# Cross-attention by Gram matrices: first loads, first batch and last row reordered, with fourteen unused products ahead of the first context

## The reference

```python
g = g_w @ c + g_b;  theta = theta_w @ x + theta_b;  phi = phi_w @ c + phi_b
W = theta.T @ phi / N
y = (W @ g.T).T
wy = w_w @ y + w_b
out = bn_gamma * (wy - bn_mean) * rsqrt(bn_var + 1e-5) + bn_beta + x
```

## Time and profile before

| | |
|---|---|
| median of 3 runs | 789.84 us (789.63 to 790.43) |
| profiled execution | 790.07 us |
| its span, first to last instruction | 788.3 us |
| PE busy | 772.0 us, 98% of the span |
| DVE, ACT, POOL busy | 498.1, 303.7, 527.5 us |
| moved by DMA | 103.17 MB, 131 GB/s over the span |
| granted TensorE clock, mean | 0.999 |

### The profile page before, as it was taken

The page is one execution under the profiler, slowest core; times in us unless marked ns, Lnnn a source line. Parts: engine busy times, 40 slices in busy tenths (PEclk is TensorE's granted clock), DMA queues, the critical chain, the costliest instruction groups (busy, mean ns, idle before and its releaser), DMA issues.

```text
span 788.3 us, 11592 instructions
## 1 busy us (share of the span) xinstructions
PE 772.0 (98%) x4045; PEld 666.7 (85%) x4045; DVE 498.1 (63%) x889; ACT 303.7 (39%) x514; POOL 527.5 (67%) x358
## 2 busy tenths in 40 slices
PE   4999999999999999999999999999999999999997
PEld 4688888888888888888888888888888888888886
DVE  3796574847657496574847657496574847657254
ACT  3634542325334243542325334243542325334131
POOL 4969785767857578585767857578585767857400
PEclk9999999999999999999999999999999999999999
DMA  9828254181733707255181733707255181730202
GB/s 237 197 108 214 107 129 192 35 226 62 178 142 74 246 0 213 106 124 195 33 228 58 178 142 72 247 0 213 106 121 198 32 228 60 178 143 1 107 1 106
DMA packets 55127, 103.17 MB, mean 131 GB/s; under 512 B 2474, under 2 KB 37956, under 8 KB 55108
## 3 DMA queue, kind: packets, MB, share of 16 engines
q1 hardware_dynamic: 52976, 101.86, 44.2%
q10 hardware_dynamic: 2132, 1.05, 0.8%
HBM read 69.35 MB, written 33.55 MB: 131 GB/s over the span
## 4 chain that ended last, share of the span: by engine, by line
PE 96%; DVE 1%; DMA 1%; ACT 1%; issue 0%; DVEq 0%; SPq 0%
PE wbank L667 57%; PE gbank L667 37%; PE wbank L830 1%; DMA ctx_sb<-in_ctx_dram 1%; PE wbank L708 1%; DVE x_sb L486 0%; PE wbank L686 0%; PE wbank L714 0%; ACT x_sb L366 0%; DVE tmp L509 0%; DVE tmp L508 0%; ACT x_hi L340 0%; DVE junk L590 0%; DVE x_sb L657 0%; DVE th_lo L583 0%
## 5 line engine op out<-in xcount | busy, mean ns | idle before, releaser
L286 POOL TENSOR_TENSOR ctxT_lo<-ctxT,ctxT_hi 128x512 fp32r<-128x512 f32 x124 | 167.2, 1349 | 205.7 <-ACT ctxT_hi L340 205.7
L297 POOL TENSOR_TENSOR ctx_sum<-ctx_sum,ctxT 128x512 f32<-128x512 f32 x108 | 157.0, 1454 | 0.2
L315 POOL TENSOR_TENSOR x_lo<-x_sb,x_hi 128x1024 fp32r<-128x1024 f32 x60 | 142.3, 2403 | 0.0
L340 ACT ACTIVATE mt<-wbank 128x512 fp32r<-128x512 f32 x64 | 37.9, 597 | 236.6 <-PE wbank L667 236.6
L657 DVE SCALAR_TENSOR_TENSOR x_sb<-wbank,const,x_sb 128x512 f32<-128x512 f32 x112 | 78.9, 747 | 73.1 <-PE wbank L667 73.1
L667 PE MATMUL wbank<-ctxT_lo,ctxT_hi 128*128 128x512 f32 x512 | 121.6, 393 | 0.0
L518 DVE TENSOR_TENSOR stage<-gbank,mt 128x384 f32<-128x384 f32 x64 | 28.3, 486 | 139.7 <-PE gbank L667 139.7
L667 PEld LDWEIGHTS wbank<-ctxT_lo,ctxT_hi 128*128 128x128 f32 x512 | 95.5, 190 | 18.7 <-POOL ctxT_lo L286 0.2
L340 ACT ACTIVATE ctxT_hi<-ctxT 128x512 fp32r<-128x512 f32 x124 | 76.5, 628 | 88.1 <-DVE ctxT L486 88.1
L667 PE MATMUL gbank<-ctxT_hi 128*128 128x384 f32 (+1 forms) x512 | 80.8, 314 | 10.1 <-ACT ctxT_hi L340 10.1
L667 PEld LDWEIGHTS gbank<-ctxT_hi 128*128 128x128 f32 x512 | 80.0, 191 | 12.0 <-issue 10.1
(11 more groups left out here) (107 smaller groups left out, 1327.4 us busy)
## 6 DMA issues: line engine op xcount, KB each, us to landing
x_sb<-in_x_dram SPq DMA_DIRECT2D x16, 2048.0 KB, 7.8
out_dram<-x_sb SPq DMA_DIRECT2D x64, 512.0 KB, 2.6
ctx_sb<-in_ctx_dram SPq DMA_DIRECT2D x60, 512.0 KB, 8.4
ctx_sb<-in_ctx_dram ACTq DMA_DIRECT2D x4, 256.0 KB, 7.1
ctx_sb<-in_ctx_dram SPq DMA_DIRECT2D x4, 256.0 KB, 7.2
x_sb<-in_L_xattn_w_w_dram SPq DMA_DIRECT2D x1, 512.0 KB, 11.7
stage<-in_L_xattn_theta_w_dram SPq DMA_DIRECT2D x1, 512.0 KB, 12.5
phi_nat<-in_L_xattn_phi_w_dram SPq DMA_DIRECT2D x1, 512.0 KB, 12.7
```

What stands on the lines that cost most here:

```text
L286: nc.gpsimd.tensor_tensor(ctxT_lo[:, c, :], turned_ctx(b, c), f(ctxT_hi[:, c, :]), ALU.subtract).then_inc(sem_, 1)
L297: nc.gpsimd.tensor_tensor(ctx_sum[:, :], ctx_sum[:, :], src, ALU.add).then_inc(ctxT_used, 1)
L315: nc.gpsimd.tensor_tensor(x_lo[:, k, :], x_sb[par][:, k, :], f(x_hi[:, k, :]), ALU.subtract).then_inc(x_lo_made, 1)
L340: nc.scalar.activation(dst, src, ACT.Copy).then_inc(sem_, 1)
```

## The change

The first context's loads are split otherwise between the two queues and go ahead of all vectors but two. gamma and var of the batch norm are loaded first, to rows of their own, turned by PE at once (`turn_norm`) and used from PSUM, so that the scale is made before the context is there. The other six vectors are loaded and turned later, after chunk 4. x of batch 0 is loaded right behind w_w. PE does 14 products of 128 x 512 ones whose result nobody reads, before it waits for the first context. DVE takes a second of the four first low parts of x from POOL. The context of batch 1 is transposed and split after T (chunks 0 to 3), after theta(1) (4 and 5) and among the first output rows (6 and 7). In the last batch the last output row is made, added up and stored in three pieces of 512, 256 and 256 columns, products of one piece after the other.

```diff
+    WARM_UP = 14
     NW = 5
...
         p1 = sb("p1", [P, KI])
-        vec_rows = sb("vec_rows", [5 * KC + 3 * KI, P])
-        vec_cols = sb("vec_cols", [P, 5 * KC + 3 * KI])
-        bt_col, bp_col, bg_col = (vec_cols[:, 5 * KC + i * KI:5 * KC + (i + 1) * KI] for i in range(3))
+        vec_rows = sb("vec_rows", [3 * KC + 3 * KI, P])
+        vec_cols = sb("vec_cols", [P, 3 * KC + 3 * KI])
+        bt_col, bp_col, bg_col = (vec_cols[:, 3 * KC + i * KI:3 * KC + (i + 1) * KI] for i in range(3))
         nbp_col = sb("nbp_col", [P, KI])
...
+        norm_rows = x_sb[1][0:2 * KC, 3, 0:P]
         theta_nat = stage[:, 0:KI * C].rearrange("p (k c) -> p k c", k=KI)
...
-        VECTORS = (w_b, bn_gamma, bn_beta, bn_mean, bn_var, theta_b, phi_b, g_b)
+        VECTORS = (w_b, bn_beta, bn_mean, theta_b, phi_b, g_b)
...
         W_BANK = [wbank[3], wbank[4]]
+        NORM_BANK = VEC_BANK = wbank[3]
         TP_BANK = [wbank[1], wbank[2], wbank[0], wbank[3]]
...
+        LAST_PIECES = [(0, HALF, wbank[1]), (HALF, HALF // 2, wbank[2]), (HALF + HALF // 2, HALF // 2, wbank[3])]
         OUT_BANK = [[wbank[1], wbank[2]], [wbank[3], gbank[0]], [wbank[4], wbank[0]], [wbank[1], wbank[2]]]
...
         vec_step = sem("vec_step")
-        vec_turned = sem("vec_turned")
+        vec_turned, vec_taken = sem("vec_turned"), sem("vec_taken")
+        in_norm, norm_turned = sem("in_norm"), sem("norm_turned")
         root_done, scale_made = sem("root_done"), sem("scale_made")
...
-            load_first_ctx(sp, (0, 2), 0)
-            load_vectors(sp, range(0, 4))
-            load_first_ctx(sp, (0, 2), 1)
+            sp.dma_start(norm_rows[KC:2 * KC, :], bn_var.rearrange("(m p) -> m p", p=P)).then_inc(in_norm, 16)
+            load_first_ctx(sp, (0, 1), 0)
+            load_first_ctx(sp, (0, 1), 1)
+            load_vectors(sp, range(0, 3))
             sp.dma_start(w_nat, w_w.rearrange("(m p) c -> p m c", p=P)).then_inc(in_w1, 16)
+            load_x(0, 0)
             sp.dma_start(theta_nat, theta_w.rearrange("(k p) c -> p k c", p=P)).then_inc(in_w4, 16)
             sp.dma_start(phi_nat[:, :, :], phi_w.rearrange("(k p) c -> p k c", p=P)).then_inc(in_w3, 16)
-            load_x(0, 0)
             sp.dma_start(g_nat, g_w.rearrange("(k p) c -> p k c", p=P)).then_inc(in_w2, 16)
...
                     load_ctx(b + 2)
-                for m in range(KC):
+                for m in range(KC if nxt else KC - 1):
                     sp.wait_ge(work_free, NO * b + NH * (m + 1))
                     sp.dma_start(out[b].rearrange("(m p) n -> m p n", p=P)[m], x_sb[par][:, m, :]).then_inc(stored, 16)
+                if not nxt:
+                    m = KC - 1
+                    for i, (a, n, bank) in enumerate(LAST_PIECES):
+                        sp.wait_ge(work_free, NO * b + (NH * m + i + 1))
+                        sp.dma_start(out[b].rearrange("(m p) n -> p m n", p=P)[:, m, a:a + n],
+                                     x_sb[par][:, m, a:a + n]).then_inc(stored, 16)
                 if nxt2:
...
             batches(sp, body)
-            sp.wait_ge(stored, 16 * KC * B)
+            sp.wait_ge(stored, 16 * (KC * B - 1 + len(LAST_PIECES)))
...
             nc.gpsimd.memset(ones_r[:, :].bitcast(F32), 1.0).then_inc(ones_done, 1)
+            nc.gpsimd.memset(x_hi[:, 0, 0:HALF].bitcast(F32), 1.0).then_inc(ones_done, 1)
...
             sum_rest(0)
-            for k in range(1, KC):
+            for k in (2, 3):
                 pool.wait_ge(x_hi_made, k + 1)
...
-            load_first_ctx(act, (1, 3), 0)
-            load_vectors(act, range(4, 8))
-            load_first_ctx(act, (1, 3), 1)
+            act.dma_start(norm_rows[0:KC, :], bn_gamma.rearrange("(m p) -> m p", p=P)).then_inc(in_norm, 16)
+            load_first_ctx(act, (2, 3), 0)
             act.wait_ge(ident_done, 2)
             nc.scalar.activation(tmp[:, 7, :], ident[:, 0:KC], ACT.Sqrt)
+            load_first_ctx(act, (2, 3), 1)
+            act.wait_ge(vec_step, 1)
+            nc.scalar.activation(tmp[:, 1, :], tmp[:, 0, :], ACT.Sqrt).then_inc(root_done, 1)
+            load_vectors(act, range(3, 6))
             hi(ident_r[:, :], ident[:, :], ident_r_made)
...
                 ctx_hi(0, c)
-                if c == 3:
-                    act.wait_ge(vec_step, 2)
-                    nc.scalar.activation(tmp[:, 1, :], tmp[:, 0, :], ACT.Sqrt).then_inc(root_done, 1)
...
             act.wait_ge(ones_done, 1)
+            act.wait_ge(vec_taken, 1)
             for k in range(KI):
...
                        LOW_BANK[g][:, 0:3 * P].rearrange("p (j c) -> p j c", j=3), low_hi_made)
-                if first(b):
-                    next_hi(0)
-                    next_hi(1)
-                    next_hi(2)
...
-                next_hi(3)
+                if not first(b):
+                    next_hi(3)
                 theta(0)
...
                 if first(b):
-                    next_hi(4)
-                    next_hi(5)
-                next_hi(6)
-                next_hi(7)
+                    for c in range(RING):
+                        next_hi(c)
+                else:
+                    next_hi(6)
+                    next_hi(7)
                 for k in range(KI):
...
                 theta(1)
+                if first(b):
+                    for c in range(RING, CH):
+                        next_hi(c)
                 if nxt:
...
-            wb_, gamma_, beta_, mean_, var_ = (vec_cols[:, i * KC:(i + 1) * KC] for i in range(5))
+            wb_, beta_, mean_ = (vec_cols[:, i * KC:(i + 1) * KC] for i in range(3))
+            gamma_, var_ = NORM_BANK[:, 0:KC], NORM_BANK[:, KC:2 * KC]
             ve, root, r0, r2, r3, r4, wm = (tmp[:, i, :] for i in range(7))
-            dve.wait_ge(in_first[0], 16 * QT)
-            for c in range(RING):
-                transpose_chunk(0, c)
-            dve.wait_ge(vec_turned, 1)
-            chain(nc.vector.tensor_copy(vec_cols[:, :], wbank[3][:, 0:5 * KC + 3 * KI]))
+            dve.wait_ge(norm_turned, 1)
             chain(nc.vector.tensor_scalar(ve, var_, EPS, None, ALU.add))
-            dve.wait_ge(in_first[1], 16 * QT)
-            transpose_chunk(0, 4)
             dve.wait_ge(root_done, 1)
             chain(nc.vector.reciprocal(r0, root))
-            transpose_chunk(0, 5)
             chain(nc.vector.tensor_tensor(r2, r0, r0, ALU.mult))
-            transpose_chunk(0, 6)
             chain(nc.vector.tensor_tensor(r3, r2, ve, ALU.mult))
-            transpose_chunk(0, 7)
             chain(nc.vector.tensor_scalar(r4, r3, -0.5, 1.5, ALU.mult, ALU.add))
...
             nc.vector.tensor_scalar(scale[:, :], r0, 1.0 / N, None, ALU.mult).then_inc(scale_made, 1)
+            for h in range(2):
+                dve.wait_ge(in_first[h], 16 * QT)
+                for c in range(RING):
+                    transpose_chunk(0, h * RING + c)
+            dve.wait_ge(vec_turned, 1)
+            nc.vector.tensor_copy(vec_cols[:, :], VEC_BANK[:, 0:3 * KC + 3 * KI]).then_inc(vec_taken, 1)
...
             first_x_lo_part(0)
+            first_x_lo_part(1)
             dve.wait_ge(w_turned, KI)
...
                 if first(b):
-                    next_ctx()
                     dve.wait_ge(in_bp, 16)
...
                 if first(b):
+                    dve.wait_ge(vec_taken, 1)
                     chain(nc.vector.tensor_tensor(wm, wb_, mean_, ALU.subtract))
...
                     chain(nc.vector.tensor_tensor(const[:, :], r3, beta_, ALU.add))
-                    transpose_chunk(b + 1, 4)
-                    transpose_chunk(b + 1, 5)
-                if nxt:
+                    next_ctx()
+                elif nxt:
                     transpose_chunk(b + 1, 6)
...
                 theta(1)
+                if first(b):
+                    transpose_chunk(b + 1, 4)
+                    transpose_chunk(b + 1, 5)
+                def last_row(m):
+                    for i, (a, n, bank) in enumerate(LAST_PIECES):
+                        dve.wait_ge(out_done, NO * b + (NH * m + i + 1))
+                        nc.vector.scalar_tensor_tensor(out=x_sb[par][:, m, a:a + n], in0=bank[:, 0:n],
+                                                       scalar=const[:, m:m + 1], in1=x_sb[par][:, m, a:a + n],
+                                                       op0=ALU.add, op1=ALU.add).then_inc(work_free, 1)
                 for m in range(KC):
+                    if m == KC - 1 and not nxt:
+                        last_row(m)
+                        break
+                    if first(b) and m in (1, 2):
+                        transpose_chunk(b + 1, 5 + m)
                     for h in range(NH):
...
+            def turn_norm():
+                pe.wait_ge(ident_done, 2)
+                pe.wait_ge(in_norm, 16 * 2)
+                nc.tensor.transpose(NORM_BANK[:, 0:2 * KC], norm_rows, ident[0:2 * KC, 0:2 * KC]).then_inc(norm_turned, 1)
             def turn_vectors():
-                pe.wait_ge(ident_done, 2)
```

(36 more changed lines are left out.)

## The result

The changed kernel takes 783.47 us (median of 6 runs, 783.38 to 783.70), the kernel before 789.81 (6 runs, 789.52 to 790.43): 6.3 us less, a ratio of 0.992 with a 95% interval of 0.9907 to 0.9933. The profiled executions, 790.07 and 783.43, have spans of 788.3 and 781.6 us.

The account below looks back on a forecast made before the run. PE, busy 98% of the span, bounds the kernel, so only the start, first batch and end can be won: 2.4 at Z + 0.7 at T + 1.5 at the end = 4.6, giving 785.2 us, range 783.9 to 787.5.

Parts of the forecast that it names:

- the wait before W's second turn: Between W's two groups of turns, PE's 1.09 us wait for ACT's mt goes; 0.6 of it won at Z.
- POOL with the later context: Batch 1's context split later on POOL: least slack 3.3 us, nothing lost; rival that POOL bounds batch 1, chance 0.05.
- I let the context's first half land 0.4 later than 8.6, at 9.0: Start: one 2 KB load ahead of the context on each queue delays its first half by 0.4 us.
- x goes right behind w ... so 21.0: Loads of batch 0: 1 MB less ahead of x, 2.6 us at 400 GB/s, so it lands at 21.0 instead of 23.6.
- that holds the fourth turn to 26.4 and Z to 28.2: Before Z: DVE's x_lo to 25.75 and copies of W to 27.05 delay PE, so Z begins at 28.2.
- the step from the pass to Z: From the end of the first pass over context 0 to Z: 0.6 us won.
- The scale chain on DVE: Ahead of the context: steps of 0.2 us, done near 6.5 and hidden; at 1.21 each they hold the transposes by 4.
- The useless products: Start: fourteen from about 3.6 to near 9.7, then 0.8 us of waiting; chunk 0 at full pace, pass ends 1.8 earlier.
- falls back in the wait: Rival at the start: the useless products bring nothing, PE's pace being slow after 11.8; total 787.3 us, chance 0.17.
- T of the first batch: T of batch 0: the fourth block's 0.73 us wait for its bank goes, 0.7 won.
- The second x_lo on DVE: Before Z: one more x_lo on DVE, 1.87 us, ending at 25.75; without DVE holding Z, Z begins at 27.5.
- The end: After the last product: DVE ends 0.67 us earlier, the 128 KB store takes 0.7 to 1.0 less; 1.5 won.

Follow-up runs that it names:

- run 1: The changed kernel without the fourteen useless products: 785.33 us.
- run 4: The changed kernel with x of batch 0 loaded behind theta_w and phi_w again: 785.51 us.
- run 5: The changed kernel with the context of batch 1 transposed and split in its old places: 785.14 us.
- run 6: The changed kernel with the last output row made, added and stored whole, as before: 784.87 us.
- run 2: The changed kernel with the old split of context 0, quarters 0 and 2 on SP, 1 and 3 on ACT: 785.59 us.
- run 9: The kernel before with only the new split of context 0's quarters over the queues: 788.84 us against 789.72, ratio 0.9991.
- run 8: The changed kernel with the old split of context 0's quarters and 20 useless products instead of 14: 784.85 us.
- run 13: The changed kernel with quarters 0 and 3 of context 0 on SP, 1 and 2 on ACT: 785.31 us.
- run 10: The kernel before with only the fourteen useless products and their memset added: 790.03 us, ratio 1.0005.
- run 3: The changed kernel with the six other vectors issued between the two halves of context 0 again: 783.95 us.
- run 7: The changed kernel with the second low part of batch 0's x back on POOL: 785.00 us.

## Why the prediction was wrong

**The direction and most of the mechanism were right.** The unused products bring the first real ones to full pace; the wait before W's second turn goes; T's wait goes; POOL with the later context is in time; the pieces shorten the end. POOL's being in time is read from the trace; each of the others was removed by itself, and the time came back (runs 1, 4, 5, 6).

**The step that failed:** "I let the context's first half land 0.4 later than 8.6, at 9.0". It landed at 7.73. I had priced the extra load in front and entered the new deal of the quarters at nothing, without naming it. It is 1.2 us at the landing by run 2 and 1.1 by run 9 (0.8 by run 8), and it is what the loads behind it start from. The 0.4 for the extra load is neither confirmed nor refuted: with the old deal the changed kernel's context landed at 8.95 and 8.51 (runs 2 and 8), the earlier kernel's at 8.61. The second half was there at 12.8 instead of the 14.1 to 14.8 forecast.

**What followed from it:** "x goes right behind w ... so 21.0". It landed at 18.5. The 2.6 for x's new place was right (18.5 and 21.0 in the changed kernel and run 4); the base was wrong, as what stood behind the context in the queues came earlier with it: with the new deal alone the kernel before has x at 21.3 instead of 23.6 (run 9), and 2.6 less than that is 18.7. With x at 18.5 the next step, "that holds the fourth turn to 26.4 and Z to 28.2", had no ground: DVE was done with x_lo at 23.1 and waited for PE. So the step from the pass to Z gave 1.5 where 0.6 was forecast. In runs 4 and 8, where x is later, DVE holds Z at 28.1 and 27.6. The scale chain on DVE, which had a high price in my range, took 0.16 to 0.18 a step and was over at 5.3.

**The useless products** were sized well in effect, but two of their inputs were off. The norm vectors were there at 2.4, not 3.3, and the pace rose after about 3 us of them, not 5 to 6. The end came at 7.4 and the wait behind it was 1.85, not 0.8. Neither is fixed: in the traces with fourteen products they took 4.84 to 6.21 and the wait behind them was 0.56 to 1.87. My rival "falls back in the wait", 0.17, did not occur in this kernel (10 runs, mean clock 0.999 or 1.00). In its neighbours it did, by the mean clock: in 3 of 4 runs with the old split, 3 of 4 in run 13, all 10 of run 10, and 1 of 4 each in runs 3, 5 and 7 (0.997 or 0.998), which have the changed kernel's deal and nearly its landing. The length of the wait does not tell the cases apart: the clock fell behind waits of 1.52, 1.77 and 1.87 (runs 2, 10, 13) and held behind 1.79 and 1.85 (run 5's trace and the changed kernel). In the three traces where it fell the first product of the context began at 9.80 or later, in the nine with fourteen products where it held at 9.51 or earlier; a landing half a microsecond later (8.28 against 7.75) goes with the difference. The change was nearer to that rival than its six close runs tell, and that all six held is in part luck.

The Trainium skill (TensorE: Matmul & The Clock Gate, Back-to-back issue gap) gives N divided by 1.2 GHz, 0.43 for a cold 512-wide product. The trace agrees for the useless products, which start 0.43 apart while slow; the real ones in the rows before had 0.47. As the prediction said, neither decides.

**T of the first batch** was undersized: 1.0 instead of 0.7, as I took the wait's row and not the step's length (6.74 to 5.75). Against PE as early as it now is, the old place costs 1.4 at T and 1.7 by the medians (run 5).

**The second x_lo on DVE** I priced as a cost of 0.6, with no gain. It cost nothing (Z at 26.26 with it and 26.32 without), and without it PE waits for POOL, 1.15 us in the trace and 1.5 by the medians (run 7).

**The end** was right: 3.3 us behind the last product instead of 4.7. The last piece takes 0.48 on DVE (0.45 forecast) and its 128 KB are seen 2.1 us after the issue, where 512 KB took 2.6: 0.5 less, not 0.7 to 1.0. From the fit of the Trainium skill (DMA: Bandwidth & Descriptors, Anatomy of one DMA), which the page gives for transfers issued from GpSimd and not from SP, the estimates are 2.3 and 3.2, a difference of 0.9; both measured times are lower, and so is the difference.

**Batches 1 and 2** held, as forecast: the same 5.35 us stand at theta(1) of the first batch and at the start of the second, and 5.33 at the last product.

What stays open: why the split changes the rate of the load, and what exactly makes the clock fall in some executions of one program and not in others.

## What to carry to other kernels

Where a change deals the same loads to the queues in another way, that is a term of its own. At a start bounded by loads, 1 us of landing moved everything behind it, and a rate read from the trace before holds only for its deal. Idle-time products can lose again what they won in the wait behind them. Twenty in place of fourteen closed that wait, and the mean clock stayed at 1.00 in four runs of four where it had been lower in three of four. And they pay only if what they bring forward is not awaited elsewhere: in the kernel before they brought nothing in the times, since the clock fell and PE waited longer for ACT's mt. Price a move between engines against the time at which the bound engine will want it after the change, not before: POOL's x_lo had 1.1 us of slack and had none left once PE came 4 us earlier, and T's wait, 0.73 before, would have been 1.16.

## What was not expected of the hardware

- The clock fell after short waits. In run 10 PE idled for 1.77 us, did 0.8 us of products at full pace and waited 0.45; within that wait, at 10.7 us, the granted clock fell to 1.2 GHz, and it stayed there to 14.2, while PE worked from 11.07 on almost without a pause. At the end of the kernel before it stayed up for 3 us of full idleness.
- The same bytes in the same 512-byte pieces over two queues moved at 249 to 254 GB/s when each queue had one half of the partitions, and at 216 to 232 when it had two quarters of different halves.
- DVE's two x_lo took 3.50, 3.70 and 4.44 us in three of these kernels (the changed one, runs 4 and 8). POOL's sums ran beside them in all three; the cause is not shown.
